# A graph network with experts on one core: weights once an expert into four resident buffers, copied tile by tile; first norm's loads on a queue of their own; the experts' preparation inside routing

## What is computed

```
x1 = layernorm(x + hypergraph_attention(x))          # first norm; its rows times W_gc follow
gc = (segment_sum(h[src], dst) * rsqrt(deg_in)) @ W_gc + b_gc
x  = gc + (feats @ W_res + b_res)
logits = x @ Wg + bg                                 # 64 experts
vals, idx = top_k(logits, 2); gates = softmax(vals)
# rows sorted by expert; per expert e (256 -> 512 -> 256):
h1 = gelu(h @ w1[e] + b1[e]);  h2 = h1 @ w2[e] + b2[e]
y  = x + sum over the two experts of gate * h2 ;  batch norm, layernorm of x1 + y
```

## Time and profile before

| | us |
|---|---|
| median of 3 runs | 6789.0 (6785.06 to 6792.79) |
| the profiled execution | 6818.4, its span 6816.8 |
| first norm, about 4160 to 4290 | 130 |
| routing, about 5560 to 5756 | 196 |
| experts, 5756 to 6587 | 831 |
| last norm, 6587 to 6817 | 230 |

### The profile page before, as it was taken

One profiled execution on the slowest core, in us unless ns is written; L12 is line 12 of the kernel. 1 busy time (PEld: TensorE's weight loads), 2 busy tenths in 40 slices (PEclk: granted clock), 3 DMA queues, 4 the chain that ended last, 5 costly groups with the idle time before them and its releaser, 6 DMA issues. The chain is left out here.

```text
span 6816.8 us, 105162 instructions
## 1 busy us (share of the span) xinstructions
PE 4422.5 (65%) x22417; PEld 2791.1 (41%) x22464; DVE 4241.2 (62%) x8841; ACT 2123.7 (31%) x3871; POOL 3417.5 (50%) x3174
## 2 busy tenths in 40 slices
PE   6999987775333333466666665566666553889973
PEld 3455543332000000244444443444444442677751
DVE  8999988888999999666566555222222245111126
ACT  0000024446999999211111112100000001223322
POOL 1000026664555555477777772677777745011135
PEclk9999999997666666688788777777777756999985
DMA  0000027774001001256777775455454653778852
GB/s 5 17 10 9 10 62 147 147 147 111 29 27 31 27 27 30 56 95 96 94 95 96 94 93 95 139 152 153 152 153 152 211 91 123 244 245 272 282 186 80
DMA packets 370288, 730.73 MB, mean 107 GB/s; under 512 B 78008, under 2 KB 222910, under 8 KB 362016
## 3 DMA queue, kind: packets, MB, share of 16 engines
q0 software_dynamic: 146928, 357.64, 28.4%
q1 hardware_dynamic: 216080, 340.22, 15.2%
q10 hardware_dynamic: 7200, 32.03, 1.2%
HBM read 511.16 MB, written 187.14 MB: 102 GB/s over the span
## 5 line engine op out<-in xcount | busy, mean ns | idle before, releaser
L109 POOL DMA_INDIRECT slots_by_target<-pay,target_slot x831 | 950.7, 1144 | 665.7 <-PE OE L956 428.3
L1033 POOL DMA_INDIRECT rowsS<-hyperedge_rows,idxS x928 | 1032.8, 1113 | 342.3 <-issue 279.8
L1490 POOL DMA_INDIRECT rows<-h_table,idxT x928 | 968.8, 1044 | 389.5 <-issue 270.3
L1512 PE MATMUL pm<-rows,ohT 128*128 128x257 f32 x1856 | 667.6, 524 | 506.4 <-issue 316.1
L956 PE MATMUL OE<-Pb,xs 128*32 128x512 f32 (+1 forms) x2352 | 410.5, 862 | 737.7 <-DVE xs L820 737.7
L1512 PEld LDWEIGHTS pm<-rows,ohT 128*128 128x128 f32 x1856 | 471.4, 265 | 687.5 <-issue 596.5
L1565 DVE TENSOR_TENSOR ohT<-iota,edgesT 128x512 f32<-128x512 f32 x232 | 160.6, 693 | 884.0 <-PE pm L1512 833.3
L1086 PE MATMUL pmS<-rowsS,ohS 128*128 128x256 f32 x1856 | 644.1, 508 | 81.7 <-DVE rowsS L1207 75.4
L438 PE MATMUL placed_sums<-onehot_tile,onehot_row 128*128 128x464 f16 x3328 | 671.1, 360 | 0.3 <-DVE onehot_tile L505 0.3
L646 PE MATMUL running<-onehot_edge,onehot_node 128*128 128x512 bf16 (+1 forms) x2738 | 541.7, 352 | 131.9 <-SPq L578 103.9
L801 DVE SCALAR_TENSOR_TENSOR Pb<-negative_b,ai,low 128x1251 f32<-128x1251 f32 x392 | 586.6, 1517 | 14.3 <-ACT low L887 14.3
(11 more groups left out here) (335 smaller groups left out, 7295.7 us busy)
## 6 DMA issues: line engine op xcount, KB each, us to landing
w<-in_L_gnn_w_dram SPq DMA_DIRECT2D x322, 512.0 KB
expert_inputs<-zeroE SPq DMA_DIRECT2D x64, 1024.0 KB
log_counts<-snap POOLq DMA_DIRECT2D x49, 625.5 KB, 5.2
negative_log_counts<-log_counts ACTq DMA_DIRECT2D x49, 625.5 KB, 3.4
negative_log_counts<-no_edge POOLq DMA_DIRECT2D x49, 625.5 KB
log_counts_in<-negative_log_counts SPq DMA_DIRECT2D x49, 625.5 KB, 3.8
xt<-expert_inputs SPq DMA_DIRECT2D x161, 128.0 KB, 2.7
expert_outputs<-ye POOLq DMA_DIRECT2D x161, 128.0 KB, 3.9
```

The source lines that it names most:

```text
L109: self.pool.indirect_dma_start(self.table[:, :], bass.IndirectOffsetOnAxis(ap=self.slot[:, c:c + 1], axis=0), self.pay[:, c, :], None, bou ...
L1033: pool.indirect_dma_start(rows[:, n % B, q, :], None, k.OEB[:, :], bass.IndirectOffsetOnAxis(ap=idx[:, n * Q + q:n * Q + q + 1], axis=0), ...
L1490: pool.indirect_dma_start(rows[:, n % B, q, 0:FEAT], None, k.H[:, :], bass.IndirectOffsetOnAxis(ap=idx[:, n * Q + q:n * Q + q + 1], axis=0 ...
L1512: last = pe.matmul(pm[:, (u % 2) * (Q // 2) + g, 0:FEAT + 1], oh[:, u, q, :], rows[:, u, q, :], start=(q % 2 == 0), stop=(q % 2 == 1))
```

## The change

First norm: `xc` gets four buffers instead of two, SP issues only loads, and the stores of `h_rows` go to POOL, behind its copy and its clearing of `big2`. Routing takes over the experts' preparation: the loads of both biases, the split of b2, the turning of b1, and the row of the table, which now stay in memory. Experts: SP loads each expert's w1, w2 and b2 once, into buffer e mod 4 of `w1r`, `w2r` and `b2r`, as soon as the tiles of expert e - 4 have been copied out of it; DVE copies w1 and b2 of each tile's expert into a working buffer, ACT copies w2, and PE multiplies from these. The tile's rows `xt` are loaded by POOL, in the same loop as the stores. The diff, cut to what matters:

```diff
@@ phase_first_norm
-        xc = sb("xc", [P, 2, K, FEAT], F32)
+        XB = 4
+        xc = sb("xc", [P, XB, K, FEAT], F32)
...
-                if r >= 2:
-                    sp.wait_ge(s_used, r - 1)
+                if r >= XB:
+                    sp.wait_ge(s_used, r - XB + 1)
...
-            for r in range(NR):
-                if r + 2 < NR:
-                    load(r + 2)
-                store(r)
+            for r in range(2, NR):
+                load(r)
...
         @block.gpsimd
...
             pool.memset(k.big2[:, :, :], 0.0).then_inc(s_gi, 1)
+            for r in range(NR):
+                pool.wait_ge(s_h, (r + 1) * K)
+                pool.dma_start(rows(k.H, r, K), hs[:, r % 2, :, :]).then_inc(s_st[r % 2], 16)
@@ phase_route
+            sp.dma_start(b1r[:, :], k.b1[:, :]).then_inc(s_b, 16)
+            sp.dma_start(b2r[:, :], k.b2[:, :]).then_inc(s_b, 16)
             for r in range(2, NR):
                 load(r)
             sp.wait_ge(s_tab, 1)
             sp.dma_start(k.etab.rearrange("a (b p t) -> p (a b) t", p=P, b=2), t2i[:, :, :]).then_inc(s_out, 16)
+            sp.wait_ge(s_b2, 1)
+            sp.dma_start(k.b2parts[:, :, :], b2p[:, :, :]).then_inc(s_out, 16)
             sp.wait_ge(s_out, stored)
+            sp.dma_start(k.etabr[:, :], k.etab[:, :]).then_inc(s_row, 16)
+            sp.wait_ge(s_row, 16)
...
@@ phase_experts
+            for e in range(EXPERTS):
+                u = e % NB
+                if e >= NB:
+
+                    end = sp.value_load(k.eends[0:1, e - NB:e - NB + 1], min_val=0, max_val=MT)
+                    sp.wait_ge(s_c1, end * 2 + 1)
+                    sp.sem_inc(idle["sp"], 1)
+                    sp.wait_ge(s_c2, end + 1)
+                    sp.sem_inc(idle["sp"], 1)
+                sp.dma_start(w1r[:, u, :, :], k.w1[e, :, :].rearrange("(c p) n -> p c n", p=P)).then_inc(s_ld[u], 16)
+                sp.dma_start(w2r[:, u, :, :], k.w2[e, :, :].rearrange("(c p) n -> p c n", p=P)).then_inc(s_ld[u], 16)
+                sp.dma_start(b2r[:, u, :], k.b2parts[e, :, :]).then_inc(s_ld[u], 16)
+                if e:
+                    sp.wait_ge(s_ld[(e - 1) % NB], 48 * ((e - 1) // NB + 1))
+                    sp.sem_inc(s_ready, 1)
...
             def hidden(t, w):
...
-                pe.wait_ge(s_ld[w], loaded)
+                pe.wait_ge(s_c1, t * 2 + 3)
...
         @block.scalar
...
+                act.wait_ge(s_ready, e + 1)
+                act.wait_ge(s_y, t + B - 1)
+                act.sem_inc(idle["act"], 1)
+                act.activation(w2[:, u % 2, :, :], w2r[:, bass.ds(e % NB, 1), :, :].rearrange("p a c n -> p (a c) n"),
+                               ACT.Copy).then_inc(s_c2, 1)
+
                 act.wait_ge(s_h, t + 3)
...
         @block.vector
...
+            def weights(t, u):
+                e = dve.value_load(tab[0:1, bass.ds(t, 1)], min_val=0, max_val=EXPERTS - 1)
+
+                dve.wait_ge(s_ready, e + 1)
+
+                dve.wait_ge(s_h, t + 1)
+                dve.sem_inc(idle["dve"], 1)
+                dve.tensor_copy(w1[:, u % 2, :, :], w1r[:, bass.ds(e % NB, 1), :, :].rearrange("p a c n -> p (a c) n")).then_inc(s_c1, 1)
+
+                dve.tensor_copy(b2[:, u % B, :], b2r[:, bass.ds(e % NB, 1), :].rearrange("p a n -> p (a n)")).then_inc(s_c1, 1)
...
                 for u in range(B):
                     rows(i * B + u + 2, u)
+                    weights(i * B + u + 2, u + 2)
                     outputs(i * B + u, u)
...
         @block.gpsimd
...
+            def load(t, u):
+                at = pool.value_load(tab[0:1, bass.ds(t + 2 * P, 1)], min_val=0, max_val=SLOTS // P)
+                pool.dma_start(xt[:, u, :], k.xbuf[bass.ds(at * P, P), :]).then_inc(s_lx[u], 16)
...
+            for t in range(B):
+                load(t, t)
+            with pool.Fori(0, MT // B - 1) as i:
+                for u in range(B):
+                    t = i * B + u
+
+                    pool.wait_ge(s_tr, t + 1)
+                    pool.sem_inc(idle["pool"], 1)
+                    load(t + B, u)
+                    store(t, u, i * (8 * B) + 16 * (u // 2) + 16)
```

More of the change, by code:

```diff
@@ L1276, in phase_first_norm @@
         s_e = sem("target_edges_loaded")
-        s_x = [sem("xc_loaded0"), sem("xc_loaded1")]
+        s_x = [sem("xc_loaded%d" % u) for u in range(XB)]
         s_used = sem("xc_used")
@@ L1650, in phase_route @@
         s_tab = sem("expert_table_ready")
-        s_out, stored = k.stores(32)
+        s_b = sem("biases_loaded")
+        s_b2 = sem("b2_parts_ready")
+        s_bt = sem("b1_transposed")
+        s_row = sem("expert_table_row_loaded")
+        s_out, stored = k.stores(48)
         block = ctx.enter_context(nc.Block())
@@ L1733, in _ @@
             pe.matmul(pS[:, 0:E], k.ones[:, :], cum[:, (NR - 1) % 2, G, :], start=True, stop=True).then_inc(s_tot, 1)
+            pe.wait_ge(s_b, 32)
+            pe.wait_ge(s_x3T, NTILE)
+            for c in range(HID // P):
+                last = pe.transpose(p3[:, 0, c * E:(c + 1) * E], b1r[:, c * P:(c + 1) * P], k.ident[0:E, 0:E])
+            last.then_inc(s_bt, 1)
         @block.scalar
@@ L1927, in _ @@
+            sp.wait_ge(s_ld[(EXPERTS - 1) % NB], 48 * ((EXPERTS - 1) // NB + 1))
+            sp.sem_inc(s_ready, 1)
         @block.tensor
         def _(pe):
-            pe.wait_ge(s_in, loaded)
-            for c in range(HK):
-                last = pe.transpose(pT[:, 0, c * EXPERTS:(c + 1) * EXPERTS], b1r[:, c * P:(c + 1) * P],
-                                    k.ident[0:EXPERTS, 0:EXPERTS])
-            last.then_inc(s_bt, 1)
             pe.sem_inc(s_y, B)
             pe.sem_inc(s_h, 2)
-            pe.wait_ge(s_b, 1)
@@ L1969, in outputs @@
                 for c in range(HK):
-                    last = pe.matmul(pY[:, u, 0:FEAT], hT[:, u, c, :], w2[:, w, c, :], start=False, stop=(c == HK - 1))
+                    last = pe.matmul(pY[:, u, 0:FEAT], hT[:, u, c, :], w2[:, u, c, :], start=False, stop=(c == HK - 1))
                 last.then_inc(s_y, 1)
@@ L1976, in step @@
                 if hiding:
-                    hidden(t + 1, (u + 1) % B, i * 48 + (96 if u + 1 >= B else 48))
+                    hidden(t + 1, (u + 1) % B)
                 outputs(t, u)
@@ L1982, in _ @@
             turn(1, 1, 16)
-            hidden(0, 0, 48)
+            hidden(0, 0)
             with pe.Fori(0, MT // B - 1) as i:
@@ L2033, in outputs @@
                 dve.tensor_copy(y[:, u % 2, :], pY[:, u % 2, 0:FEAT]).then_inc(s_yc, 1)
-            rows(0, 0)
-            rows(1, 1)
+            for t in range(2):
+                rows(t, t)
+                weights(t, t)
             with dve.Fori(0, MT // B - 1) as i:
@@ L2042, in _ @@
                     rows(t + 2, t)
+                    weights(t + 2, t + 2)
                 outputs(t, t)
@@ L2051, in store @@
                 pool.sem_inc(idle["pool"], 1)
-                pool.dma_start(k.ybuf[bass.ds(t * P, P), :], y[:, u, :]).then_inc(s_st[u], 16)
-                pool.wait_ge(s_st[u], stored)
+                pool.dma_start(k.ybuf[bass.ds(t * P, P), :], y[:, u % 2, :]).then_inc(s_st[u % 2], 16)
+                pool.wait_ge(s_st[u % 2], stored)
                 pool.sem_inc(s_yfree, 1)
-            with pool.Fori(0, MT // 2) as i:
-                for u in range(2):
-                    store(i * 2 + u, u, i * 16 + 16)
-            store(MT - 1, 0, 16 * (MT // 2) + 16)
+            for t in range(B):
+                load(t, t)
+            with pool.Fori(0, MT // B - 1) as i:
+                for u in range(B):
+                    t = i * B + u
[3 more added lines that the diff above has]
+                    store(t, u, i * (8 * B) + 16 * (u // 2) + 16)
+            for t in range(MT // B * B - B, MT):
+                if t + B < MT:
+                    pool.wait_ge(s_tr, t + 1)
+                    load(t + B, t % B)
+                store(t, t, 16 * (t // 2) + 16)
 def phase_last_norm(nc, k):
```

99 lines of the change are left out of this document (40 added, 59 removed).

## The result

| | before | after |
|---|---|---|
| median of the runs (11 each, same chip) | 6788.05 us | 6806.24 us |
| span of the profiled execution | 6816.8 us | 6793.9 us |
| stores of the tiles: first, last start | 5783.3, 6579.9 | 5718.0, 6552.4 |
| step of a tile (160 steps) | 4.98 us | 5.21 us |
| landing of a store, mean of 161 | 3.96 us | 2.80 us |

The ratio is 1.004 with a 95% interval of 1.002 to 1.0059: some 27 us more, 14 to 40. The median stands 18 us higher. The forecast was 6821 us, 32 more than before, in a range of 6726 to 6900. So the spans must not be compared, but stages can be.

What follows compares the result with a forecast made beforehand. The prediction took POOL's wait in place for each store's landing as the bound. Tiles +69, preparation -10 and first norm -27 summed to +32 us, taking the median from 6789 to 6821 us, range 6726 to 6900.

Steps and rivals of the forecast that it cites:

- POOL's chain is the bound: Experts' tiles before the change: landing of a store plus about 1.0 us of POOL's own work sets the 4.98 us step.
- First norm, -27 us: First norm: four of DVE's five waits for `xc` go, 28.5 us, less 1.5 for the last store by POOL.
- Preparation, -10 us: Start of the experts: first weights issued at once instead of 9.95 us in, routing hiding the rest; bounds -7 to -11.
- Rest 2.55 us: POOL's tile loop beside the landing: 1.0 us grows by 0.7 for the table read and 0.84 for issuing `xt`.
- Landing 2.86 us: Tiles' stores: 2.0 us alone plus 0.40 x 1.9 for fewer weights, plus 0.1 for `xt`; bounds 2.1 and 3.9.
- Step 5.41, tiles +69 us: Tile loop: 2.55 + 2.86 us instead of 4.98, over 160 steps; bounds -118 and +266 us.
- `hidden` waiting for w1's copy or `xTe`: Sign in the tiles that the prediction is right: `hidden` waits for these, not for a load.
- the experts don't change: Rival, tiles: POOL's two loop terms cancel at 5.13 to 5.30 us a tile; 6775 to 6803 us, chance 0.16.
- the case that I held likeliest: Tiles: the longer step, 5.3 to 5.7 us, giving 6821 us; chance 0.43.
- The shorter landing: Rival, tiles: most stores land in 2.0 to 2.3 us, step 4.6 to 4.9, -74 us, 6715; chance 0.26.
- The copy that holds POOL up: Rival, tiles: DVE's w1 copy delays POOL's `xt` issue by 0.5 us a tile, +111 us, 6900; chance 0.12.
- PE takes over: Rival, tiles: POOL's loop under 4.14 us, so PE sets the step, -171 us, 6618; chance 0.03.

Runs made afterwards that it cites:

- the first two experiments: The kernel before with the changed first norm alone, then with the changed preparation too and the tile loop of before: ratios 0.9972 and 0.9948.
- the loop of before: The kernel before with the changed first norm and preparation, its own tile loop kept (weights for every tile, `xt` by SP): ratio 0.9948.
- the kernel with nothing else changed: The kernel before with only the loads of `xt` moved to POOL, weights still loaded for every tile: ratio 1.0143, step 5.55 us.
- the group of 7107 us: The second four follow-up kernels, measured on a chip where the kernel before had a median of 7107 us.
- the store first: The changed kernel with POOL issuing the store ahead of the table read and `xt`, then waiting for the landing: ratio 1.015, step 5.75 us.

## Why the prediction was right in its number, and where it was not

- *POOL's chain is the bound.* Shown: taking the wait out of the chain gave PE's 4.18 us.
- *First norm, -27 us.* -29.0 to the next phase's first gather in the trace of after, -27 to -29 in the first two experiments. The 28.5 us of waits came back as worked out (31.3 to 3.0). The 1.5 us for the last store by POOL were due too: the end of the phase takes 1.6 us more, though the store itself landed in 4.7 us against 4.9 on SP. Why the phase is some 2 us shorter than the two make it is not shown.
- *Preparation, -10 us.* -7.8 with the loop of before. In after it is -6.3 (5686.7 to 5718.0, 31.3 us instead of 37.6); there the first tile needs the two copies as well, an explanation that I didn't try apart. Routing hides what it took over, as forecast.
- *Rest 2.55 us* (its terms add up to 2.54). 2.41. Table read and issue of `xt` were within 0.14 us of their estimate, also in the kernel with nothing else changed.
- *Landing 2.86 us.* 2.80, and this is the right number by a wrong rule. I took the landing as linear in the megabytes for each tile. Same bytes gave 3.15, 3.48, 3.96 and 5.06 us in four kernels, by the place at which the weights fall. In after it is a mixture: 45 stores with weights issued within 3 us ahead of them or 1 us behind land in 4.3 us, the other 116 in 2.2.
- *Step 5.41, tiles +69 us.* 5.21, +38 between the two traces (32 to 51 against the other traces of the same loop). Rest and landing were each a little short of the estimate.
- *The end of the experts' phase, nothing.* +4.9 us. The prediction had no term for it: POOL's DRAIN takes 8.95 us with `xt` on POOL and 4.05 without.
- *Sum +32 us.* The medians give +18, the ratio 14 to 40. The traces give -29.0 - 6.3 + 37.8 + 4.9 = +7 for the changed parts, or +2 to +21 with the steps of the other traces of the loop of before. So that the time came out within 15 us is in part luck: the tiles cost 31 us less than forecast, and the measured terms leave some of the measured difference open. The spans hold a further -30 in stages whose code didn't change, 24 of them ahead of the first norm. Other traces of that same code start the first norm at 4143 to 4165 us on three chips (the group of 7107 us left out), against 4163 and 4138 here, so I take this for the spread between executions.
- *Signs.* Right: the landing, the first norm, the first weights at once, the copies as long as assumed (w1's 0.69 us, w2's 1.06). Wrong: "POOL's stores 5.3 to 5.7 us apart" (5.21), "`ye` still waiting for POOL's line" (9.0 us in 4 pieces were left) and "`hidden` waiting for w1's copy or `xTe`". Behind the landing stands `xt`'s issue, and PE waits for `xt`. I had counted what POOL's new instructions add to POOL's own step, and not who waits for the transfer that they issue. The step came out because POOL's chain is the same length either way. The same omission made me expect a gain from the store first, where it cost 1.5% against the kernel before.
- *Rivals.* The measured step is that of the rival "the experts don't change" (5.13 to 5.30 us, chance 0.16), and not of the case that I held likeliest; it is also the step that I had worked out as the turning point, at which the kernel would be level. It is slower all the same; 4.9 us of that are POOL's DRAIN. The shorter landing could have outrun the loop, for with no weights at all the step is 4.50 us, but the rival's 4.6 to 4.9 asks for landings of 2.2 to 2.5 on average with the measured rest, and 45 stores that meet a load make it 2.80. (That rival counted 1.3 us for table read and `xt`, where the sum has 1.54; 1.39 were measured.) The copy that holds POOL up is real, with 0.09 us a tile, not 0.5: most issues miss it. PE takes over only where `xt` or the wait leaves POOL's chain.

## What to carry to other kernels

An engine that waits in place for its own transfer puts everything it issues next on the path, with its full duration: let the wait stand one step later, before adding work to that engine. Work out for each moved transfer not only what its issue costs but who needs the data and how far ahead it now starts. And before saving bytes, look where in the step they go out; 1 MB just ahead of a small store cost 1.5 us of landing that the same megabyte just behind it didn't.

## What the runs showed of the hardware that was not expected

- A 128 KB store by POOL lands in 2.0 to 2.3 us alone, 3.5 with 1 MB issued on SP's queue 0 to 2 us behind it, and 5.0 to 5.2 with it 0 to 2 us ahead. The Trainium skill, "DMA: Bandwidth & Descriptors", section "Queues, rings and completion order", says that a DMA engine takes turns between its queues by packets; by that alone the store would not stand behind the megabyte that was issued first. The rows show 3 us more than alone, about what a megabyte takes at the 313 GB/s of the busiest stretch (3.4 us, an estimate). Why is not shown.
- DMA busy at 0.97 of its share and 313 GB/s left PE busy for 617 of 620 us.
- PE's 16 matmuls took 3.35 us after a wait of 3.06 us, 1.95 otherwise; the granted clock was 0.50 (1.2 GHz) directly behind that wait. Over all tiles of after it is 0.95, against 1.00 where PE has no such waits.
- POOL's DRAIN at the end of the experts' phase took 4.04 or 4.05 us with 161 transfers issued by POOL in the phase and 8.95 to 9.03 with 322.
- The issue of seven tiles' rows takes POOL 0.93 us, of one tile's 0.54.
- Issuing `xt` on ACT's queue took 0.35 us against 0.54 on POOL, and ACT, busy 412 of 620 us, didn't become the bound: PE was busy for 613.
